# Scatter, expert blocks, gathers and sums of a mixture-of-experts layer, moved from three stages into one

## The reference, cut to what matters

```python
# first mixture (layer 0): hidden width 256
logits = tokens @ router_w.T;  rw, re = top_k(softmax(logits), 2);  rw = rw / rw.sum(-1)
out = tokens
for e in range(8):
    h = gelu(tokens @ w1[e] + b1[e]);  y = h @ w2[e] + b2[e]
    out = out + combine[:, e:e+1] * y
x = x + out                    # tokens = layernorm(x)

# second mixture (layer 1): hidden width 1024, its own layer norm with gain and bias per expert
h = gelu(xe[e] @ W1[e] + b1[e]);  y = h @ W2[e] + b2[e]
x = x + (weights * y[selected]).sum(1)
```

## Time and profile before

| | |
|---|---|
| median of three runs | 3072.06 us |
| profiled execution | 3073.55 us, its span 3071.8 us |
| TensorE matmul busy | 2293.7 us (75%) |
| VectorE busy | 1512.9 us (49%) |
| ScalarE busy | 1199.8 us (39%) |
| GpSimd busy | 700.6 us (23%) |
| mean granted TensorE clock | 0.895 |
| HBM read and written | 286.88 MB and 77.05 MB, 118 GB/s over the span |
| 50 + 50 scatters, line 1669 | 96.7 us busy, 967 ns each |
| 50 + 50 gathers, line 1698 | 97.4 us busy, 974 ns each |

### The profile page before, as it was taken

The page is one execution under the profiler, slowest core; times in us unless marked ns, Lnnn a source line. Parts: engine busy times, 40 slices in busy tenths (PEclk is TensorE's granted clock), DMA queues, the critical chain, the costliest instruction groups (busy, mean ns, idle before and its releaser), DMA issues. The chain is left out here.

```text
span 3071.8 us, 49968 instructions
## 1 busy us (share of the span) xinstructions
PE 2293.7 (75%) x10879; PEld 1802.4 (59%) x10880; DVE 1512.9 (49%) x3026; ACT 1199.8 (39%) x2471; POOL 700.6 (23%) x719
## 2 busy tenths in 40 slices
PE   2777776888888868964195399977999234999990
PEld 1344443666666647854174288866888233888880
DVE  6788875888888873346033645342010540111113
ACT  1788843777777732231021132223222311222220
POOL 0000011777777710020502411000100023000006
PEclk9999997999999999985598699988999656999995
DMA  5311122777777710000286322202222022555544
GB/s 217 144 64 64 64 76 86 210 213 213 213 213 213 213 42 33 0 3 24 98 262 189 108 67 63 78 26 81 70 69 67 2 96 98 195 200 181 204 158 130
DMA packets 186915, 364.52 MB, mean 119 GB/s; under 512 B 55682, under 2 KB 139063, under 8 KB 182135
## 3 DMA queue, kind: packets, MB, share of 16 engines
q1 hardware_dynamic: 141352, 218.24, 22.0%
q0 software_dynamic: 45520, 145.80, 16.5%
HBM read 286.88 MB, written 77.05 MB: 118 GB/s over the span
## 5 line engine op out<-in xcount | busy, mean ns | idle before, releaser
L1981 PE MATMUL gnn_p<-gnn_y,gnn_counts_wide 128*128 (+1 forms) x2500 | 554.0, 381 | 2.6 <-DVE R_kept L1916 2.4
L1981 PEld LDWEIGHTS gnn_p<-gnn_y,gnn_counts_wide 128*128 128x128 f32 x2500 | 473.0, 191 | 69.5 <-DVE R_kept L1916 6.9
L851 POOL DMA_INDIRECT kv_pair<-kv,gather_idx x448 | 426.5, 952 | 151.2 <-issue 107.0
L1852 ACT CAST gnn_counts_wide<-gnn_counts 128x1664 f32<-128x1664 uint16 x100 | 157.8, 1579 | 422.8 <-PE gnn_p L1981 404.6
L951 PE MATMUL p_edge_q<-QX_kept,onehot_turned 128*128 x904 | 264.3, 416 | 62.5 <-ACT onehot_turned L914 59.9
L951 PEld LDWEIGHTS p_edge_q<-QX_kept,onehot_turned 128*128 128x128 f32 x904 | 155.5, 191 | 165.4 <-issue 149.7
L558 PE MATMUL adj_p<-adj_onehot_src,adj_onehot_key 128*128 128x416 f16 x1200 | 237.1, 348 | 10.0 <-DVE adj_onehot_src L532 7.5
L959 PE MATMUL p_sums<-R_kept 128*128 128x264 f32 x896 | 237.3, 388 | 0.0
L1698 POOL DMA_INDIRECT combine_y<-slots_out,CSLOT x100 | 97.4, 974 | 611.6 <-DVE CSLOT L1730 581.7
L1347 ACT ACTIVATE experts_hidden<-experts1p_hidden,pack 128x256 f32<-128x256 f32 x232 | 110.0, 474 | 303.8 <-PE experts1p_hidden L1376 303.8
L1376 PE MATMUL experts1p_hidden<-experts_turned,pack 128*128 128x256 f32 x928 | 206.9, 381 | 1.2 <-DVE experts_turned L1300 1.2
(11 more groups left out here) (323 smaller groups left out, 3328.0 us busy)
## 6 DMA issues: line engine op xcount, KB each, us to landing
pack<-experts SPq DMA_DIRECT2D x27, 2052.0 KB, 8.2
gnn_counts<-adj SPq DMA_DIRECT2D x400, 104.0 KB, 2.2
adj<-adj_counts SPq DMA_DIRECT2D x100, 208.0 KB, 1.9
experts_rows<-slots_in SPq DMA_DIRECT2D x60, 256.0 KB, 4.5
slots_out<-experts_y SPq DMA_DIRECT2D x58, 256.0 KB, 4.9
pack<-experts SPq DMA_DIRECT2D x27, 513.0 KB, 4.1
experts_rest<-experts SPq DMA_DIRECT2D x60, 130.0 KB, 4.6
kv_pair<-kv,gather_idx POOLq DMA_INDIRECT x448, 3.8
```

Source lines behind the costliest of these rows:

```text
L851: pool.indirect_dma_start(kv[r][:, j, :], None, a["kv"], bass.IndirectOffsetOnAxis(ap=idx[r][:, j:j + 1], axis=0)).then_inc(kv_in[r], 16)
L1852: act.copy(wide[b][:], raw[r][:].rearrange("p q s -> p (q s)")).then_inc(wide_ready, 1)
L1981: mm = pe.matmul(bank[:, off:off + D], wide[b][:, j * P:(j + 1) * P], y[:, at(n), :].squeeze(1), start=first and off == 0, stop=last and ( ...
```

## The change

Scatter, blocks, gathers and sums of a layer become one stage, `experts(k, layer)`, and the feed-forward network gets a function of its own, `ffn_blocks`, with the same instructions as before.

- **Slots by tile.** `moe_route` now counts an expert's rows tile by tile: two matmuls with 200 columns (prefix over the partitions and total, for each expert and tile) take the place of two with 8 columns. A block then holds the tokens of a few neighbouring tiles.
- **An order of blocks.** `Order` (33 VectorE instructions, one waiting for the other, and 4 small matmuls) computes for each block the first and the last tile that it holds, and sorts the blocks by the last. It writes three tables: `ORDER` (place of the block and its expert), `WHEN` (how many groups of four tiles, `GN`, have to be scattered before the block's rows may be loaded) and `NEED` (for each group of tiles, after how many pairs of blocks its results may be gathered).
- **Scatter.** GpSimd issues the same 50 scatters and counts up `landed` for each group of four tiles whose scatters have landed. SyncE's queue runs a small loop before each load of rows: it waits for `landed` to be 1, 2, ... up to the block's `WHEN`.
- **Gathers.** After the scatters GpSimd gathers group by group. Before each group it runs a loop over `NEED` pairs that waits for the stores of those blocks. In layer 0 it first adds `X` to the normalised rows in one instruction of 128 x 6400, in place of two VectorE instructions per tile.
- **Sums.** VectorE's sums come after all blocks, in the same stage. Layer 0 has two sums and the statistics per tile, where there were four sums and the statistics.
- The loads of the first two packs wait for `Order`'s end. `block_of` and `WHEN` are read from memory by SyncE's queue for each block.

```diff
+NB = NBLK + 2
+GN = 4
+NGRP = -(-NT // GN)
...
-            link(dve.tensor_tensor_scan(cum[:].rearrange("p e t -> p (e t)"), member[:].rearrange("p e t -> p (e t)"),
+            dve.tensor_tensor(member[:].rearrange("p e t -> p t e"), hit1[:], hit2[:], ALU.add).then_inc(cnt_ready, 1)
+            dve.wait_ge(sums_ready, 1)
+            totals, prefix = pTot[:, 0:NEXP * NT], pPre[:, 0:NEXP * NT]
+            link(dve.tensor_tensor_scan(cum[:].rearrange("p e t -> p (e t)"), totals,
                                         nought[:, 0:1].to_broadcast([P, NEXP * NT]), 0.0, ALU.add, ALU.add))
             link(dve.tensor_copy(ends[:, 1:NEXP + 1], cum[:, :, NT - 1]))
...
+            link(dve.tensor_tensor(before[:].rearrange("p e t -> p (e t)"), cum[:].rearrange("p e t -> p (e t)"), totals,
+                                   ALU.subtract))
+            link(dve.tensor_tensor(before[:].rearrange("p e t -> p (e t)"), before[:].rearrange("p e t -> p (e t)"), prefix,
+                                   ALU.add))
+            link(dve.tensor_tensor(slot[:], before[:].rearrange("p e t -> p t e"),
                                    adj[:].unsqueeze(1).to_broadcast(byexp), ALU.add))
...
+class Order:
...
+    def vector(self, dve):
...
+        link(dve.tensor_scalar(self.limit[:], pid, float(BT), float(BT), ALU.mult, ALU.add))
+        link(dve.tensor_scalar(self.cut[:, 0, :], k["ADJ"][:], -1.0, self.limit[:, 0:1], ALU.mult, ALU.add))
+        link(dve.scalar_tensor_tensor(out=self.cut[:, 1, :], in0=self.cut[:, 0, :], scalar=-float(BT), in1=ends,
+                                      op0=ALU.add, op1=ALU.min))
+        link(dve.tensor_tensor(self.cut[:, 0, :], self.cut[:, 0, :], ends, ALU.min))
...
+        link(dve.tensor_scalar(self.seen[:, 0, :], run, self.edge[:, 0:1], None, ALU.is_lt))
+        link(dve.tensor_scalar(self.seen[:, 1, :], run, self.edge[:, 1:2], None, ALU.is_le))
+        link(dve.tensor_reduce(self.count[:], self.seen[:], AX.X, ALU.add))
...
+        link(dve.tensor_scalar(self.key[:], self.tiles[:, 0:1], float(P), pid, ALU.mult, ALU.add))
+        link(dve.scalar_tensor_tensor(out=self.key[:], in0=self.past[:], scalar=float(64 * P), in1=self.key[:],
+                                      op0=ALU.mult, op1=ALU.add))
+        dve.tensor_scalar(self.diag[:], ident, self.key[:, 0:1], None, ALU.mult).then_inc(self.diag_ready, 1)
...
+        dve.wait_ge(self.keys_ready, 1)
+        link(dve.tensor_scalar(self.less[:], self.p_keys[:, 0:NB], self.key[:, 0:1], None, ALU.is_lt))
+        link(dve.tensor_reduce(self.pos[:], self.less[:], AX.X, ALU.add))
...
+        dve.wait_ge(self.rows_done, 1)
+        link(dve.tensor_copy(k["ORDER"][:], self.p_rows[0:1, 0:NB]))
+        link(dve.tensor_copy(self.first[:], self.p_rows[0:1, NB:2 * NB]))
+        link(dve.tensor_copy(k["WHEN"][:], self.p_rows[0:1, 2 * NB:3 * NB]))
...
+        link(dve.tensor_reduce(self.need[:], self.by[:], AX.X, ALU.max))
+        link(dve.tensor_scalar(self.need_i[:], self.need[:], 2.0, None, ALU.max))
+        dve.tensor_scalar(k["NEED"][:], self.need_i[:], 1, None, ALU.arith_shift_right).then_inc(self.ready, 1)
...
+def block_of(nc, engine, k, j):
+    word, = table_values(nc, engine, k["ORDER"], j, [511])
+    why = "the chip computed the table within these bounds"
+    return (nc.s_assert_within(word & 63, 0, NB - 1, skip_runtime_bounds_check_because=why),
+            nc.s_assert_within(word >> 6, 0, NEXP - 1, skip_runtime_bounds_check_because=why))
...
+def experts(k, layer):
...
+            def load_rows(j, b, used):
+                slot, e = block_of(nc, mybir.EngineType.SP, k, j)
+                group = sp.value_load(k["WHEN"][0:1, at(j)], min_val=1, max_val=NGRP)
+                wait_if(sp, turned, used)
+                sp.sem_inc(tally, 1)
+                with sp.Fori(0, group) as g:
+                    sp.wait_ge(landed, g + 1)
+                    sp.sem_inc(tally, 1)
+                sp.dma_start(rows[b][:], slots_in[at(slot)].squeeze(0)).then_inc(rows_in[b], 16)
+                return e
...
+            def store(j, b, ready):
+                slot, _ = block_of(nc, mybir.EngineType.SP, k, j)
+                sp.wait_ge(y_ready, ready)
+                sp.sem_inc(tally, 1)
+                sp.dma_start(slots_out[at(slot)].squeeze(0), y[b][:]).then_inc(y_out[b], 16)
+            def step(j, b, i, first, last):
+                e = load_rows(j, b, j - 1)
+                if not first:
+                    sp.wait_ge(y_done, j - 1)
+                    sp.sem_inc(tally, 1)
+                    sp.dma_start(pack[b][:, 0:G], a[name][at(e), :, 0:G].squeeze(0)).then_inc(pack_in[b], 16)
+                    store(j - 2, b, j - 1)
+                load_rest(e, b)
+            sp.wait_ge(order.ready, 1)
             for b in range(2):
-                e, = table_values(nc, mybir.EngineType.SP, k["BLOCKEXP"], b, [NEXP - 1])
-                sp.dma_start(k["PACK"][b][:], a[f"experts{layer}"][at(e)].squeeze(0)).then_inc(k["PACK_IN"][b], 16)
-        @block.vector
-        def _(dve):
-            for n in range(NT):
-                dve.tensor_scalar(rows[:, n, :], X[:, n, :], rstd[:, n:n + 1], nmr[:, n:n + 1], ALU.mult,
-                                  ALU.add).then_inc(rows_ready, 1)
+                _, e = block_of(nc, mybir.EngineType.SP, k, b)
+                sp.dma_start(pack[b][:], a[name][at(e)].squeeze(0)).then_inc(pack_in[b], 16)
+            n = over_blocks(sp, step)
+            e = load_rows(2 * n + 1, 1, 2 * n)
+            store(2 * n - 1, 1, 2 * n)
+            load_rest(e, 1)
...
+            for n in range(NT):
+                pool.wait_ge(normed_ready, n + 1)
...
+                                            normed[:, n, :], None).then_inc(scattered[n // GN], 16)
+                if n % GN == GN - 1 and n >= GN:
+                    pool.wait_ge(scattered[n // GN - 1], 16 * TOPK * GN)
+                    pool.sem_inc(landed, 1)
+            for g in range(NT // GN - 1, NGRP):
+                pool.wait_ge(scattered[g], 16 * TOPK * min(GN, NT - GN * g))
+                pool.sem_inc(landed, 1)
+            pool.wait_ge(order.ready, 1)
+            if not layer:
+                pool.tensor_tensor(normed[:], normed[:], X[:, 0:NT, :], ALU.add).then_inc(residual, 1)
+            pool.wait_ge(slots_ready, 2)
+            for g in range(NGRP):
+                pairs = pool.value_load(k["NEED"][0:1, g:g + 1], min_val=1, max_val=NBLK // 2)
+                with pool.Fori(0, pairs) as i:
+                    pool.wait_ge(y_out[0], 16 * (i + 2))
+                    pool.wait_ge(y_out[1], 16 * (i + 1))
+                    pool.sem_inc(tally, 1)
+                for n in range(GN * g, min(GN * g + GN, NT)):
+                    for j in range(TOPK):
+                        pool.indirect_dma_start(back[:, n, j, :], None, a["slots_out"], bass.IndirectOffsetOnAxis(
+                            ap=k["CSLOT"][:, n, j:j + 1], axis=0)).then_inc(back_in[n], 16)
...
+                dve.wait_ge(back_in[n], 16 * TOPK * (layer + 1))
+                if not layer:
+                    dve.wait_ge(residual, 1)
+                dve.scalar_tensor_tensor(out=sums[n % RING][:], in0=back[:, n, 0, :], scalar=k["W12"][:, n, 0:1],
+                                         in1=X[:, n, :] if layer else normed[:, n, :], op0=ALU.mult,
+                                         op1=ALU.add).then_inc(first_done, 1)
+                dve.scalar_tensor_tensor(out=X[:, n, :], in0=back[:, n, 1, :], scalar=k["W12"][:, n, 1:2],
+                                         in1=sums[n % RING][:], op0=ALU.mult, op1=ALU.add).then_inc(x_ready, 1)
+            for n in range(NT):
+                dve.tensor_scalar(normed[:, n, :], X[:, n, :], rstd[:, n:n + 1], nmr[:, n:n + 1], ALU.mult,
+                                  ALU.add).then_inc(normed_ready, 1)
+            order.vector(dve)
+            dve.tensor_scalar(k["CSLOT"][:], k["SLOT"][:], float(NSLOT), None, ALU.is_lt).then_inc(slots_ready, 1)
+            dve.wait_ge(slots_ready, 1)
+            dve.tensor_tensor(k["CSLOT"][:], k["CSLOT"][:], k["SLOT"][:], ALU.mult).then_inc(slots_ready, 1)
+            half = [0]
+            copy_turned(0, 0)
+            over_blocks(dve, step)
+            parts = (add_first, add_second) if layer else (add_first, add_second, spread_of)
...
+            order.tensor(pe)
+            half = [0]
+            turn(0, 0)
+            over_blocks(pe, step)
...
-        size = k["a"][f"experts{layer}"].shape[2]
-        k["PACK"] = [s.enter_context(nc.sbuf_tensor(f"pack{layer}_{b}", [P, size], F32)) for b in range(2)]
-        k["PACK_IN"] = [s.enter_context(nc.semaphore(f"pack_in{layer}_{b}")) for b in range(2)]
-        moe_scatter(k, layer)
-        mlp_blocks(k, f"experts{layer}", (D, FFN)[layer], True, layer == 1)
-        moe_combine(k, layer)
+        experts(k, layer)
```

(24 more changed lines are left out.)

437 lines of the change are left out of this document (226 added, 211 removed).

## The result

The changed kernel takes 2971.55 us (median of 4 runs, 2967.39 to 2985.05) against 3073.47 for the kernel before (median of 4, one more than stood ahead of the prediction): ratio 0.9675, 95% interval 0.9643 to 0.9707. It is faster, and 2971.55 lies in the predicted range, 15.5 us above the predicted 2956. The profiled execution took 2967.39 us with a span of 2965.3.

What follows compares the result with a forecast made beforehand. Serial scatters and gathers idle TensorE, which bounds layer 1's blocks; in layer 0's, TensorE and DMA are both close. Layer 0 -41.1 and layer 1 -74.6 make -115.7 from 3071.8: median 2956 us, 8-in-10 range 2922 to 2990.

Steps and rivals of the forecast that it cites:

- Blocks of layer 0: Layer 0's blocks: 166 us against 135, a cost of about 30, with bounds of 7 and 46.
- (b): SyncE's queue in layer 0's blocks: reads and loops before the rows make blocks 4.9 us early, 6.0 late.
- (a): DMA in layer 0's blocks: scatters or gathers beside some 12.5 blocks leave about 0.65 of the engines, 5.8 us a block.
- Front of layer 0: First normalisation to first turn in layer 0: 35.2 us instead of 73.9, after 24 scatters are issued; gain 38.6.
- Front of layer 1: First normalisation to first turn in layer 1: 37.5 us instead of 74.3, rows queued behind the packs; gain 36.8.
- End of layer 0: After layer 0's last bias: 40.9 us instead of 74.9, with GpSimd loops of 5.8 each before two gather groups; gain 34.
- End of layer 1: After layer 1's last bias: 27.5 us instead of 69.8, with 26 gathers and three GpSimd loops (17.0); gain 42.3.
- (1): Loops and DMA cost nearly nothing: layer 0's blocks +7 instead of +30, whole 2922 us; chance 0.15.
- (2): Loops at 0.5 us a turn or reads at twice the price: +16 in the blocks, whole 2980 us; chance 0.15.
- (3): TensorE, waiting more in layer 0, falls to half clock: its blocks take 249 us, whole 3039; chance 0.05.
- (4): Gathers wait to the end because an early group needs a late block: both ends stay, whole 3026 us; chance 0.04.
- (5): SP and GpSimd backward branches refetch code: from 0.88 us a turn the gain is gone; 3098 at 1.0; chance 0.03.

Runs made afterwards that it cites:

- e11_packs: Against e8_pool, the second block's weights are loaded behind the first block's rows instead of ahead of them; 2916.99 us.
- e6_late: Against e11_packs, every group of gathers waits for the last block in both layers, while scatters stay beside the blocks; 2990.76 us.
- e8_pool: Changed kernel with single waits for SyncE's loops, group number packed into ORDER, stores issued by ScalarE, and two waits replacing GpSimd's loop before each gather group; 2921.84 us.
- e2_twice: Against the changed kernel, SyncE's loop of WHEN turns runs twice in a row before each load of rows; 3040.81 us.
- e7_once: Against the changed kernel, a second loop that always runs one turn stands ahead of SyncE's loop of WHEN turns; 2996.47 us.
- e10_pad: Against e11_packs, VectorE repeats a statistic 8 times into its own tile behind the last one of layer 0; 2915.21 us (one run).
- e9_atonce: Against e8_pool, GpSimd counts a group of scatters as landed right behind its own last scatter, not one group later; 2919.04 us.

## Why the prediction was right, and where it was off

**Verdict and place.** The gain comes from the four ends and is partly paid for in layer 0's blocks, as the sum had it. All four ends gave more than predicted, 166.7 us against 151.7, and layer 0's blocks took 62.9 against 30. That the total came out 9 us from the sum is in part luck: the blocks' 62.9 lie beyond the prediction's own upper bound of 46, and of their error of 33 us the ends gave back 15 and the rest (layer 1's blocks, routing, other stages) some 9.

**Blocks of layer 0, the term that was mis-sized.** The mechanism (b), SyncE's queue, was right; its cycle was counted too short. The step reads "2.6 from pack issue to rows issued, 0.2 more for a loop turn, and 3.2 are 6.0". Three things are missing late, at `WHEN` 7. The way from rows issued to the next pack issued isn't in it: 0.30 us when nothing is waited for (1650.57 to 1650.87). The loop takes 2.70 us, not 7 x 0.33, which is 0.39 more. And the read of `ORDER` ahead of the rows was priced at 0.27 us, the median of all such reads before; in its place behind the issues of store and rest it takes 0.72 in the mean over layer 0's blocks, 0.45 more. One of them, at 1660.3:

```profile
L430 SPq TENSOR_LOAD <-ORDER x1: 646/646/646, 1660.3 to 1660.3; - x1
```

6.0 + 0.30 + 0.39 + 0.45 = 7.1, against 7.3 in the three blocks shown and 7.5 in the mean of all at `WHEN` 7. The same cycle bounds the early blocks: 6.3 us at `WHEN` 3, where the sum took 5.1, or 5.8 beside scatters. The 26 spacings from the fourth block's rows on add up to 178.7 us; 13.4 us more pass before them and 6.2 behind the last. The upper bound of 46 was broken because it rested on the same short cycle.

**DMA contention (a)** was sized well and then hidden under (b). The sum had 5.5 blocks beside scatters 1.14 us dearer (6.3 us) and 7 beside gathers the same (8.0 us). The gathers measured 8.8, but beside blocks of 5 us in e11_packs and not in the changed kernel. For the scatters, 141.2 less the 135.4 of before leaves 5.8; this is argued, since e6_late differs from the kernel before in its SyncE queue too.

**Front of layer 0**: 29.1 for 35.2. The step "when GpSimd has issued the 24 scatters" failed: the queue's lead lets the count come with the 20th. The mean time of a scatter was right.

**Front of layer 1**: 36.6 for 37.5, with the rows behind the packs, as e11_packs shows.

**End of layer 0**: the last statistic at 31.5 for 40.9. Loops of 5.8 us each on the path were wrong: they take that time and more in the queue, but the queue's lead covers it. But the stage's end was not in the sum at all: 9.5 us pass from the last gather to the next stage, and VectorE's 4.4 us behind it, which I took for the end, lie inside them. The two errors go against each other, and 5.1 us more gain than predicted remain.

**End of layer 1**: 22.9 for 27.5. The bound is VectorE's 25 x 0.92 = 23.0, named in the prediction as 24 at most; That GpSimd's loops are hidden here too fits e8_pool, whose end of layer 1 is the same 22.9.

**Routing and the GpSimd addition**: nothing for +1.5 a layer; the first normalisation of layer 0 starts at 1450.97, before at 1451.06, and all that lies between the mixtures, layer 1's routing with it, takes 766.9 us against 769.3. The addition runs from 1519.41 to 1533.13, and the first gather, which waits for stored blocks, starts at 1543.23.

**Rivals.** (1) was half right: GpSimd's loops are free here, SyncE's are not. (2), dearer loops or dearer reads, was the nearest in the blocks, and both of its parts were true in part: 0.38 a turn, and 0.72 for one of the reads. (3), half clock: the granted clock fell from 0.98 to 0.92 in the blocks, and to 0.82 in e2_twice with TensorE waiting more, but TensorE was never the limit; it was busy 69% of the stretch (136 of 198). The prediction's 67% doesn't follow from its own 166 us, which give 122 / 166 = 73%, and the 7.6 us a block at half clock are too few: 122.11 / 29 x 0.98 / 0.50 is 8.3. (4) didn't happen. (5) needed 0.88 us a turn; the dearest turn in any run here takes 0.60.

**The register read.** The sum went by the trace's 272 ns and not by the floor of about 600 ns that the Trainium skill gives (DMA: Bandwidth & Descriptors, section Latency and other measured facts). The trace refutes the floor: the reads of `ORDER` and `WHEN` have medians of 273 and 268 ns and a least of 261. But the median was the wrong figure to take, since the read of `ORDER` ahead of the rows takes 0.72 us in the mean of 28.

Open is why GpSimd's `DRAIN` ends 9.2 us behind the start of the last gather here, in e6_late too, when in the combine of the kernel before it ended 5.3 us behind it (1713.9 + 19.4 = 1733.3):

```profile
1728.05 0.94 POOL L1698 DMA_INDIRECT combine_y<-slots_out,CSLOT  x1 [0.30 <-issue]
```

## What to carry to other kernels

Count the cycle of an issuing queue once around, from one load to the same load of the next block, with every wait taken as over. That is its floor. What is added to a queue that is the bottleneck, as in e2_twice, is paid in full (67.7 us of time for 69.3 of loops). Read such a cycle from the distance between the queue's records, and in the place where the instruction stands: the median of a read over the whole kernel, or the price of a loop that two runs seem to give, can both mislead. A loop whose turns only count up to a value in a register can be one wait against that register where its value is bounded above zero: that alone was worth 43 us here. Work in a queue that runs far ahead of its engine was free here, and the same kind of work in a queue that never got ahead was not.

## What the runs showed of the hardware

A dynamic loop on SyncE with one wait and one increment in it costs 0.38 us a turn and nothing beside its turns in the changed kernel (0.78 us for 2 turns, 2.70 for 7). The recorded durations in a turn (register operation 35 ns, wait and increment 17, addition 33, branch 45) come to 0.13 us, so the durations don't price a loop; the distance from turn to turn does. In e7_once and e2_twice the same turns took 0.59 to 0.60 us in one of two copies of the code, and why is open.

The Trainium skill, Advanced Engine Details and Errata, section Control Flow Timing, gives about 108 ns for a compare-and-branch. The trace's record has 45 ns, and by either the branch explains less than a third of a turn.

A read of one table value into SyncE's register took 0.27 us at the median, and 0.72 in the mean behind the issues of a store and a load.

GpSimd's queue executed waits, counts and loops while its engine still worked through transfers of 1.26 us each. Two loops of 14 turns, 0.46 to 0.48 us a turn, showed as 0.3 to 0.6 us of idle engine. Where no loop held it, the queue reached the end of the stage 10 to 12 gathers ahead of its engine (12 in the kernel before, 10 in e10_pad). A wait for the newest transfers used up that lead and left 2.2 to 5.5 us of dry engine (e9_atonce).

32 gathers beside blocks with a DMA share of 0.86 cost these blocks 8.8 us, 0.28 each (e6_late against e11_packs), and 1.26 us each where nothing ran beside them.
